# Key sums of an attention block's first pass: plain fp32 products instead of products of high and low parts

## The reference, cut to what matters

```python
q = rope((x @ Wq + bq).reshape(b, l, 16, 16))
k = rope((x @ Wk + bk).reshape(b, l, 16, 16))
v = (x @ Wv + bv).reshape(b, l, 16, 16)
score = einsum('blhd,bmhd->bhlm', q, k) / 4
ctx = einsum('bhlm,bmhd->blhd', score, v)
out = ctx @ Wo + bo
```

## Time and profile before

| what | value |
|---|---|
| median of 3 runs | 835.01 us |
| the three runs | 835.01, 830.82, 836.17 us |
| span of the profiled execution, first to last instruction | 735.2 us |
| mean granted TensorE clock over the span | 0.950 |
| first pass, from the first product of `project` to the first load of queries | 310.9 to 404.5 us |

### The profile page before, as it was taken

The page is one execution under the profiler, slowest core; times in us unless marked ns, Lnnn a source line. Parts: engine busy times, 40 slices in busy tenths (PEclk is TensorE's granted clock), DMA queues, the critical chain, the costliest instruction groups (busy, mean ns, idle before and its releaser), DMA issues.

```text
span 735.2 us, 13758 instructions
## 1 busy us (share of the span) xinstructions
PE 607.9 (83%) x3900; PEld 535.9 (73%) x3901; DVE 450.3 (61%) x1106; ACT 357.7 (49%) x788; POOL 414.5 (56%) x444
## 2 busy tenths in 40 slices
PE   2991489999999999788997799459999999999600
PEld 2891378888888888767776699448888888888500
DVE  6427946555555555388885588684555555555256
ACT  3884424545455544378875244233545455454300
POOL 2555565777777773369996100007677777775400
PEclk9999999999999999999999999659999999999955
DMA  9666032322232231434431442113222333222199
GB/s 320 228 223 163 1 119 77 96 95 94 96 100 99 96 96 51 144 117 140 161 101 57 144 159 100 59 1 94 82 96 91 98 100 97 93 94 78 47 330 354
DMA packets 52017, 88.00 MB, mean 120 GB/s; under 512 B 15634, under 2 KB 31425, under 8 KB 51468
## 3 DMA queue, kind: packets, MB, share of 16 engines
q1 hardware_dynamic: 21334, 43.69, 17.6%
q0 software_dynamic: 13664, 35.42, 15.3%
q10 hardware_dynamic: 16982, 8.43, 3.9%
HBM read 53.96 MB, written 35.39 MB: 122 GB/s over the span
## 4 chain that ended last, share of the span: by engine, by line
PE 62%; DVE 12%; POOL 9%; DMA 9%; issue 4%; ACT 3%; SPq 1%; ACTq 0%; DVEq 0%; POOLq 0%
PE ps L836 15%; PE ps L838 15%; PE ps L837 15%; PE ps L827 11%; DMA work<-y_dram 4%; PE ps L854 3%; PE ps L831 3%; POOL aT_lo L526 2%; POOL xn_lo L520 2%; DVE xs L1385 1%; POOL work L516 1%; DMA xn_dram<-work 1%; POOL work L517 1%; DVE work L1299 1%; DMA work<-xn_dram,gidx 1%
## 5 line engine op out<-in xcount | busy, mean ns | idle before, releaser
L487 POOL DMA_INDIRECT y_dram<-work,sidx x142 | 142.8, 1006 | 72.5 <-issue 42.2
L479 POOL DMA_INDIRECT work<-xn_dram,gidx x142 | 146.2, 1029 | 46.3 <-issue 42.2
L827 PE MATMUL ps<-cst,work 128*128 128x128 f32 x824 | 132.4, 286 | 25.6 <-ACT work L586 17.2
L827 PEld LDWEIGHTS ps<-cst,work 128*128 128x128 f32 x824 | 104.8, 150 | 39.3 <-issue 15.8
L836 PE MATMUL ps<-up_hi,xT_hi 128*128 x284 | 118.1, 416 | 1.0 <-DVE xT_lo L1329 1.0
L838 PE MATMUL ps<-up_hi,xT_lo 128*128 x284 | 112.0, 395 | 0.0
L837 PE MATMUL ps<-up_lo,xT_hi 128*128 x284 | 111.9, 394 | 0.0
L686 ACT ACTIVATE work<-ps 128x256 f32<-128x256 f32 x142 | 54.7, 385 | 107.9 <-PE ps L838 107.9
L1344 DVE TENSOR_SCALAR work<-ps 128x256 f32<-128x256 f32 x142 | 59.7, 420 | 66.0 <-ACT work L686 65.4
L695 ACT ACTIVATE work<-ps,slot_gate 128x256 f32<-128x256 f32 x142 | 59.8, 472 | 81.2 <-PE ps L838 81.2
L1326 DVE SCALAR_TENSOR_TENSOR slot_gate<-work,sign,second 128x1 f32<-128x1 f32 x142 | 25.5, 219 | 100.7 <-ACT xT_hi L672 100.7
(11 more groups left out here) (164 smaller groups left out, 1394.6 us busy)
## 6 DMA issues: line engine op xcount, KB each, us to landing
work<-y_dram SPq DMA_DIRECT2D x32, 512.0 KB, 5.2
xs<-L_attn_x SPq DMA_DIRECT2D x4, 1024.0 KB, 10.4
work<-L_ffn_gate_up_proj SPq DMA_DIRECT2D x8, 512.0 KB
q_dram<-work ACTq DMA_DIRECT2D x16, 256.0 KB, 2.5
work<-q_dram SPq DMA_DIRECT2D x16, 256.0 KB, 2.7
out<-xs SPq DMA_DIRECT2D x16, 256.0 KB, 5.9
xn_dram<-work SPq DMA_DIRECT2D x16, 255.0 KB, 3.8
xn_dram<-work ACTq DMA_DIRECT2D x16, 255.0 KB, 2.2
```

The costliest lines, as they stand in the source:

```text
L479: pool.indirect_dma_start(xg[:, k, u, 1:H + 1], None, xn_dram[n], bass.IndirectOffsetOnAxis(ap=gidx[:, 2 * s + u:2 * s + u + 1], axis=0)). ...
L487: pool.indirect_dma_start(y_dram[n], bass.IndirectOffsetOnAxis(ap=sidx[:, 2 * s + u:2 * s + u + 1], axis=0), ysb[:, k, u, :], None, bounds ...
L827: ins = nc.tensor.transpose(ps[:, bank, k:k + P], src[:, u, c * P:(c + 1) * P], ident)
```

## The change

The split of both operands of the key sums goes. PE multiplies the normalised rows in `xn_a` by the rotated keys in `qk` as they are, in plain fp32: 4 products per group in the place of 12. With it go `xn_high` and `k_high` on ACT, the four subtractions of POOL's step, and `key_low` on DVE for the last two groups. `qk_out` now waits for the key sums of two groups earlier to be done (they read `qk` itself), and `normalise` for those of four groups earlier. On ACT `qk_out` moves behind `xT_high` and the square root, and `store_q` takes over the wait for the rotation. The second pair of buffers that the expert blocks borrowed from the rows' split becomes one of its own.

```diff
             def first_pass(g, j, it):
-                b = j % 2
-                last = isinstance(g, int) and g >= NG - 2
-                if not last:
...
-                pool.wait_ge(xn_hi, g + 1)
-                for u in range(2):
-                    ins = nc.gpsimd.tensor_tensor(xn1[1][:, b, u, 0:H], xn_a[:, j, u],
-                                                  xn1[0][:, b, u, 0:H].bitcast(F32), ALU.subtract)
-                ins.then_inc(xn_lo, 1)
-                if not last:
-                    pool.wait_ge(k_hi, g + 1)
-                    for u in range(2):
-                        ins = nc.gpsimd.tensor_tensor(aT[1][:, u].rearrange("p c k -> p (c k)"), qk[:, b, u, H:2 * H],
-                                                      aT[0][:, u].rearrange("p c k -> p (c k)").bitcast(F32), ALU.subtract)
-                    ins.then_inc(k_lo, 1)
...
             def qk_out(g, b, k):
                 wait(act, q_stored[b], 16 * k)
-                wait(act, k_lo, g - 1)
+                wait(act, g_used, g - 1)
...
             def store_q(g, b):
+                act.wait_ge(rot_done, g + 1)
                 act.dma_start(pair(q_dram, g), qk[:, b, :, 0:H]).then_inc(q_stored[b], 16)
...
-            def key_sums(g, b, first=False, last=False):
-                pe.wait_ge(xn_lo, g + 1)
-                pe.wait_ge(k_lo, g + 1)
+            def key_sums(g, j, first=False, last=False):
+                pe.wait_ge(rot_done, g + 1)
                 for u in range(2):
-                    k_u = [t[:, u].rearrange("p c k -> p (c k)") for t in aT]
                     for c in range(KC):
-                        o = ps[:, 6 + c, 0:H]
-                        hi, lo = [t[:, b, u, c * P:(c + 1) * P] for t in xn1]
-                        nc.tensor.matmul(o, hi, k_u[0], start=first and u == 0, stop=False, skip_group_check=True)
-                        nc.tensor.matmul(o, hi, k_u[1], start=False, stop=False, skip_group_check=True)
-                        ins = nc.tensor.matmul(o, lo, k_u[0], start=False, stop=last and u == 1, skip_group_check=True)
+                        ins = nc.tensor.matmul(ps[:, 6 + c, 0:H], xn_a[:, j, u, c * P:(c + 1) * P],
+                                               qk[:, j % 2, u, H:2 * H], start=first and u == 0,
+                                               stop=last and u == 1, skip_group_check=True)
                 ins.then_inc(g_used, 1)
```

More of the change, by code:

```diff
@@ L169, in build @@
         aT = [sb(f"aT_{h}", [P, 2, KC, P], F32R) for h in ("hi", "lo")]
-        xn1 = [sb(f"xn1_{h}", [P, 2, 2, H], F32R) for h in ("hi", "lo")]
+        aT2 = [sb(f"aT2_{h}", [P, 2, KC, P], F32R) for h in ("hi", "lo")]
         cst = sb("cst", [P, NCONST], F32)
@@ L226, in build @@
         ysb = area(4616, RING, 2, H)
-        aTb = [[t[:, :, :, :] for t in aT],
-               [t[:, :, :, :].rearrange("p b u h -> p (b u h)")[:, 0:2 * KC * P].rearrange(
-                   "p (u c t) -> p u c t", u=2, c=KC) for t in xn1]]
+        aTb = [[t[:, :, :, :] for t in pair] for pair in (aT, aT2)]
         ybuf = area(0, 4, 2, TOPK, H)
@@ L310, in build @@
         qk_ps, qk_sb, rot_parts, rot_done = sem("qk_ps"), sem("qk_sb"), sem("rot_parts"), sem("rot_done")
-        xn_hi, xn_lo, rot_cos = sem("xn_hi"), sem("xn_lo"), sem("rot_cos")
-        k_hi, k_lo, g_used = sem("k_hi"), sem("k_lo"), sem("g_used")
+        rot_cos, g_used = sem("rot_cos"), sem("g_used")
         q_stored = [sem("q_stored_a"), sem("q_stored_b")]
@@ L508, in first_pass @@
             def first_pass(g, j, it):
-                b = j % 2
-                last = isinstance(g, int) and g >= NG - 2
-                if not last:
[L512 to L517, removed]
-                pool.wait_ge(xn_hi, g + 1)
-                for u in range(2):
-                    ins = nc.gpsimd.tensor_tensor(xn1[1][:, b, u, 0:H], xn_a[:, j, u],
-                                                  xn1[0][:, b, u, 0:H].bitcast(F32), ALU.subtract)
-                ins.then_inc(xn_lo, 1)
-                if not last:
-                    pool.wait_ge(k_hi, g + 1)
-                    for u in range(2):
-                        ins = nc.gpsimd.tensor_tensor(aT[1][:, u].rearrange("p c k -> p (c k)"), qk[:, b, u, H:2 * H],
-                                                      aT[0][:, u].rearrange("p c k -> p (c k)").bitcast(F32), ALU.subtract)
-                    ins.then_inc(k_lo, 1)
+                if isinstance(g, int) and g >= NG - 2:
+                    return
+                v = qk[:, j % 2].rearrange("p u (h j c) -> p u h j c", j=HD // 2, c=2)
+                pool.wait_ge(rot_cos, g + 1)
+                pool.wait_ge(rot_parts, g + 1)
+                r, i = v[:, :, :, 0:ROT, 0], v[:, :, :, 0:ROT, 1]
+                nc.gpsimd.tensor_tensor(r, r, rotr, ALU.subtract)
+                nc.gpsimd.tensor_tensor(i, i, roti, ALU.add).then_inc(rot_done, 1)
             stages(pool, first_pass)
@@ L745, in qk_out @@
                 ins.then_inc(qk_sb, 1)
-            def xn_high(g, j):
-                wait(act, g_used, g - 1)
-                nc.scalar.activation(xn1[0][:, j % 2, :, 0:H], xn_a[:, j], ACT.Copy).then_inc(xn_hi, 1)
             def scale_cos(g, b):
@@ L771, in first_pass @@
                 if not (static and g >= NG):
-                    wait(act, xn_lo, g - 3)
+                    wait(act, g_used, g - 3)
                     normalise(A, xn_a[:, j], g, b, first=1)
                 if not (static and g < 2):
-                    xn_high(g - 2, (j + 2) % 4)
                     scale_cos(g - 2, b)
-                if not (static and not 1 <= g <= NG):
-                    qk_out(g - 1, 1 - b, it * 2 + (j - 1) // 2)
                 if not (static and g >= NG):
@@ L783, in first_pass @@
                     sqrt_var(A, 1 - b, g + 1)
+                if not (static and not 1 <= g <= NG):
+                    qk_out(g - 1, 1 - b, it * 2 + (j - 1) // 2)
                 if not (static and g < 2):
-                    k_high(g - 2, b)
                     store_q(g - 2, b)
@@ L1024, in first_pass @@
                 if not (static and g < 3):
-                    key_sums(g - 3, (j + 1) % 2, first=static and g == 3, last=static and g == NG + 2)
+                    key_sums(g - 3, (j + 1) % 4, first=static and g == 3, last=static and g == NG + 2)
             keep_running(80)
@@ L1424, in rotate_whole @@
                 v.tensor_tensor(i, i, roti, ALU.add).then_inc(rot_done, 1)
[L1426 to L1429, removed]
             def first_pass(g, j, it):
@@ L1454, in _ @@
                 rotate_whole(g, g % 2)
-                key_low(g, g % 2)
             dve.wait_ge(out_w_loaded, 64)
```

## The result

The changed kernel is faster: 825.53 us in the median of 4 runs (823.37 to 828.0) beside 834.01 of 4 runs of the kernel before; the ratio is 0.9885, with a 95% interval of 0.9853 to 0.9916. Forecast were 831.2 us, a gain of 3.8; measured were 8.5 by the medians and 9.6 by the ratio (0.0115 x 834).

The account below looks back on a forecast made before the run. POOL was taken to bound steady steps of the first pass, PE next at 5.21 us; 3.7 from 12 steps - 0.2 at the start + 0.3 at the end = 3.8, so 835.01 goes to 831.2 us, range 827.5 to 835.8.

Parts of the forecast that it names:

- POOL is the bound before: First pass, steady steps: POOL busy 5.28 of 5.52 us per step, its subtractions never waiting, so it sets the pace.
- I take 0.233, the row of equal length.: Key sums on PE: each plain fp32 instruction of 256 columns priced at 0.233 us, like a 512-column fp32r one.
- The key sums' term: PE's key sums per group after the change: 1.94 us against 1.51 before, making PE's step 5.21.
- The 0.08 for the first product: Key sums on PE: 0.08 us extra for a group's first product, from 0.20 instead of 0.12 before.
- The ring at 4.95: First pass: loop `project`, transposes, `xT_high`, `xT_low`, next `project` takes 4.95 us per step, the next floor below PE's.
- cheaper products: Key sums on PE: a plain product under 0.42 us drops steps to 4.95, total 827.8 us; chance 0.12.
- The new wait is covered by the move on ACT: First pass: `qk_out` waits for key sums of g-3, yet delays neither `normalise` (0.5 us spare) nor `xT_low` (0.2).
- the cover of 0.2 us: First pass, DVE: `xT_low` of g+1 can start at 9.2 us and is due at 9.36.
- a new wait takes POOL's place: First pass: loop via key sums, `qk_out`, rotation, `xT_low` reaches 11.04 us per two steps; 834.5 to 835.5; chance 0.14.
- My sign for it: Profile after: idle time of PE before `project`, ended by `xT_lo`, would show the new wait's loop binding.
- The end of the pass: From `project` of group 15 to the loads of queries: 11.49 us falls to 11.1, store last; 0.3 booked.
- The start: First pass: step from group 2 to 3 slows from 5.01 to 5.21 us, a loss of 0.2; earlier steps unchanged.

Follow-up runs that it names:

- e2: Kernel before, with POOL's subtraction for the keys' low part cut from 256 to 8 columns per tile; 829.74 us beside 835.15, ratio 0.9934.
- e4: Kernel before, with only ACT's copy of queries and keys moved behind `xT_high` and the square root; 736.52 us beside 737.8, ratio 0.9988.
- e5: Changed kernel, with each of the four plain products issued twice; 757.11 us beside 737.8 for the kernel before, ratio 1.0259.
- e6: Changed kernel, with five bursts of fp32r and plain fp32 products added ahead of the first pass to time them; 747.58 us, bursts included.
- e1: Changed kernel, with key sums of only one tile of two, so 2 plain products per group; 822.58 us beside 835.15, ratio 0.9839.
- e3: Changed kernel, with ACT's copy of queries and keys back ahead of `xT_high`; 868.1 us beside 835.15 for the kernel before, ratio 1.0415.
- e0: Kernel before, run again unedited for its profile; 830.0 us with a span of 828.1.
- e9: Kernel before, run again unedited for a profile on another chip; 737.06 us with a span of 735.3.

## Why the prediction was wrong, point by point

- **POOL is the bound before** (5.28 of 5.52): right. e2 took 1 us of POOL's step away and the steps fell to 5.09; e4 left it, and the steps stayed at POOL's own 5.35 to 5.4.
- **The step that failed: "I take 0.233, the row of equal length."** The key sums' term, 8 x 0.233 + 0.08 = 1.94, measures 1.73; PE's step is 4.96 (e5) and not 5.21. I had priced a plain fp32 instruction by an fp32r instruction of as many cycles, but fp32r has a surcharge of its own (0.231 for 512 columns, where two passes over 256 take 0.216, e6). The bound from below that I wrote down, 0.44/2 = 0.22 from the same operation and length at half clock, was the better row; the other one of the same operation, 0.115 for 128 columns, doubled to 0.23 and misled. The 0.08 for the first product was not there either: the chain has 1.73 from transposes to `project`. The 13 steps from group 2 on take 60.03 + 4.91 = 64.94 us instead of 13 x 5.21 = 67.73, which is 2.8 us of the gain that I missed.
- **Trainium skill.** The formula in "TensorE: Matmul & The Clock Gate", Back-to-back issue gap, that I set aside (columns/2.4 plus 2.5 ns) gives 0.218 for two passes of 256 columns, and the rows show 0.216; for plain products it came out and my choice did not. For fp32r of 512 columns it gives 0.216 against 0.231 in e6: there the trace disagrees. The section of the Trainium skill gives this formula for isolated matmuls, and for the stream of a real kernel some 131 ns per matmul of 512 columns; no burst of e6 comes near that (0.231 and 0.429).
- **The ring at 4.95**: right (4.92, e1). So the gain stopped where both floors meet, and the rival "cheaper products", which put the result at 827.8, was the case that came; I had priced it, with 0.12 for it. I had set its condition at under 0.42 per product and 4.95 per step; 0.43 and 5.00 brought 2.8 of its 3.4 us.
- **The new wait is covered by the move on ACT**: right in the main, and the move is of more weight than I saw (e3). But the cover of 0.2 us was too thin: four of the 12 steps are late by it, 0.45 us in all. That is the beginning of the rival "a new wait takes POOL's place": I summed 9.9 us for its ring over two steps, and the pairs in which it shows take 10.0 to 10.1 (5.17 + 4.96, 5.04 + 4.94, 5.15 + 4.96, 5.04 + 4.95). My sign for it, an idle time of PE ended by `xT_lo`, stands in the rows of PEld and not in those of PE.
- **The end of the pass**: 0.3 booked, 0.7 measured (10.83 for 11.49; e0 had 11.7 and e9 11.9). The form was right, with the last store at the end.
- **The start**: the step from group 2 to 3 takes 4.91, not 5.21; it is the same term again.
- **Where the rest is**: steps 13 x 0.49 = 6.3 and the end 0.7 make 7.0, less data that came late for the first steps in most profiles after. The measured 8.0 and 9.6 have 1 to 3 us more, not assigned.
- **The range** was built on the pitch as if it were sure, but that term alone did not break it: with the steps as measured the sum gives 831.2 - 2.8 = 828.4, inside. From there to the measured 825.53, 0.4 are the end of the pass, 1.0 is that the median of the kernel before moved from 835.01 to 834.01 with its fourth run, and 1.5 are not assigned. The lower end of 827.5 left nothing for such scatter under the rival's 827.8, so that a part of the miss is the luck of the runs.
- **The span** was misread by 99.8 us, which cost nothing in the sum but hid that the profile and the runs came from different chips.

## What to carry to other kernels

Price an operation by its own kind at another clock or size before you price it by another kind of equal length; where two such rows differ by 8%, carry both into the range times the number of steps. When one engine is relieved, work out every other floor (here the ring at 4.92 and PE at 4.96, both met) and check the wait that the change adds in the order of the queue: the same removal of work is 1% faster or 4% slower by the place of one copy. Split products of three fp32r matmuls cost PE less than a plain fp32 product (1.43 against 1.73 us here), so the plain form pays only if the splitting itself is what binds.

## What the runs showed of the hardware

- A plain fp32 product is two matmul instructions of two cycles per column each: 0.429, 0.216 and 0.112 us per instruction for 512, 256 and 128 columns at full clock; fp32r takes one cycle per column with 8 to 12% on top (0.231 and 0.119 for 512 and 256).
- One program took 735 us on one chip and 830 on another, and all of it in the two expert stretches (217 against 261 and 238 against 285 us), at a granted clock of 0.99 to 1.00 in the first of them on both; the 12 steps of the first pass were equal to 0.1 us in 66.2.
- Operations of DVE and POOL with both inputs in SBUF lengthened each other, and the one that came second paid. In the first profile, where a subtraction of POOL had begun 0.01 to 0.17 us before DVE's add of 512 numbers, the add took 1.12 to 1.31 us instead of 0.68 (14 of 26) and the subtraction 0.73 to 0.76; where the subtraction began with the add or up to 0.02 us behind it, the add took 0.68 and the subtraction 1.26 to 1.29 (10). In the changed kernel all 29 adds took 0.68 to 0.69. Of the 48 subtractions of the 12 steps, 16 took 1.18 to 1.29 instead of 0.72 to 0.76: an estimated 16 x 0.5/12 = 0.7 us of POOL's 5.28 per step was this, and not subtracting.
